# A transformer block in float32 pairs: new instruction orders on five engines, from the first LayerNorm to the first layer-two product

## The reference

```python
h = tok(x)                                    # shifted patches, LayerNorm, 3840 -> 192
h = h + attn(layernorm(h))                    # 12 heads of 16; keys: every 8th token, itself, its predecessor
h = h + ffn(layernorm(h))                     # 8 experts, the two likeliest of a router, 192 -> 768 -> 192
# attention: a = softmax(where(mask, q k^T / 4, -inf)); out = a v; then a 192x192 projection
# experts:   out += w_e * (gelu(x w1[e] + b1[e]) w2[e] + b2[e]),  w = top two of softmax, normalised
```

## Time and profile before

| what | value |
|---|---|
| median of 3 runs | 186.79 us (186.65 to 186.85) |
| the profiled execution: its time, its span | 186.15 us, 184.4 us |
| TensorE products busy | 172.6 us, 94% of the span |
| VectorE busy | 138.7 us, 75% |
| ScalarE busy | 116.1 us, 63% |
| GpSimd busy | 84.0 us, 46% |
| chain that ended last, by engine | PE 63%, DVE 5%, POOL 3% |

### The profile page before, as it was taken

How to read it: one execution, slowest core, us unless ns; L and a number is a source line. 1 busy time by engine, 2 the same in 40 slices (tenths; PEclk the granted TensorE clock), 3 DMA queues, 4 the chain that set the end, 5 groups by cost and what they waited for, 6 DMA issues and landing times.

```text
span 184.4 us, 3458 instructions
## 1 busy us (share of the span) xinstructions
PE 172.6 (94%) x1129; PEld 147.5 (80%) x1129; DVE 138.7 (75%) x311; ACT 116.1 (63%) x208; POOL 84.0 (46%) x111
## 2 busy tenths in 40 slices
PE   5898999698988989899999999999999999999994
PEld 2486589586865659789899899999999999999994
DVE  5479998678359973997787688688688688687553
ACT  2499653585416445756876875875975975973730
POOL 7876403521998216901651651661662562560000
PEclk9999999999999999999999999999999999999999
DMA  5999999100116800054005406406406400000002
GB/s 120 241 334 324 231 243 241 34 2 0 46 42 211 259 5 0 0 164 136 4 0 174 125 0 177 122 2 170 128 0 202 97 2 0 0 4 0 0 0 85
DMA packets 14979, 18.08 MB, mean 98 GB/s; under 512 B 2467, under 2 KB 10776, under 8 KB 14966
## 3 DMA queue, kind: packets, MB, share of 16 engines
q1 hardware_dynamic: 14422, 17.90, 35.5%
q10 hardware_dynamic: 544, 0.03, 0.2%
HBM read 17.14 MB, written 0.39 MB: 95 GB/s over the span
## 4 chain that ended last, share of the span: by engine, by line
PE 63%; DVE 5%; POOL 3%; issue 1%; POOLq 0%; DVEq 0%
PE ps L371 30%; PE ps L1187 18%; PE ps L1189 8%; PE ps L1237 1%; PE ps L1236 1%; PE ps L1235 1%; DVE merge L1268 1%; PE ps L383 1%; DVE big_r L1268 1%; POOL h L589 1%; POOL halo L597 1%; DVE bn L1435 1%; PE ps L378 1%; POOL halo L602 1%; POOL wsplit L330 1%
## 5 line engine op out<-in xcount | busy, mean ns | idle before, releaser
L371 PE MATMUL ps<-big_r,wsplit 128*128 128x512 f32 (+1 forms) x245 | 61.5, 387 | 0.0
L793 ACT ACTIVATE early<-ps,b1t 128x512 f32<-128x512 f32 x48 | 32.8, 683 | 29.1 <-PE ps L371 27.4
L1187 PE MATMUL ps<-wsplit,big_r 128*128 128x384 f32 x168 | 49.7, 355 | 0.7 <-DVE big_r L1268 0.7
L1268 DVE TENSOR_TENSOR big_r<-early,big_r 128x512 fp32r<-128x512 f32 x48 | 35.9, 750 | 15.8 <-ACT big_r L334 15.4
L371 PEld LDWEIGHTS ps<-big_r,wsplit 128*128 128x128 f32 x245 | 41.9, 189 | 6.3
L1189 PE MATMUL ps<-wsplit,big_r 128*128 128x192 f32 x168 | 42.1, 251 | 0.0
L1187 PEld LDWEIGHTS ps<-wsplit,big_r 128*128 128x128 f32 x168 | 31.5, 188 | 2.7 <-issue 1.1
L1189 PEld LDWEIGHTS ps<-wsplit,big_r 128*128 128x128 f32 x168 | 32.0, 190 | 1.3
L334 ACT ACTIVATE big_r<-early 128x512 fp32r<-128x512 f32 x48 | 30.4, 632 | 1.5
L1606 DVE SCALAR_TENSOR_TENSOR merge<-sq,gates,merge 128x192 f32<-128x192 f32 x32 | 26.9, 863 | 0.0
L316 POOL TENSOR_TENSOR wsplit<-stage,wsplit 128x768 fp32r<-128x768 f32 x4 | 7.4, 1848 | 19.3 <-ACT wsplit L334 15.7
(11 more groups left out here) (239 smaller groups left out, 282.0 us busy)
## 6 DMA issues: line engine op xcount, KB each, us to landing
stage<-in_L_ffn_w SPq DMA_DIRECT2D x4, 576.0 KB, 6.2
early<-in_L_ffn_w SPq DMA_DIRECT2D x4, 576.0 KB, 5.3
shifted<-in_L_tok_w SPq DMA_DIRECT2D x6, 288.0 KB, 7.0
early<-in_x SPq DMA_DIRECT2D x6, 256.0 KB, 4.8
stage<-in_L_ffn_w SPq DMA_DIRECT2D x4, 384.0 KB, 3.8
stage<-in_L_ffn_w SPq DMA_DIRECT2D x8, 192.0 KB, 4.8
early<-in_L_ffn_w SPq DMA_DIRECT2D x4, 384.0 KB, 3.1
early<-in_L_ffn_w SPq DMA_DIRECT2D x8, 192.0 KB, 4.2
```

The lines of the kernel that those rows point to most:

```text
L371: mm = nc.tensor.matmul(dst, lhs, rhs, start=(first and n == 0), stop=(last and n == 4))
L793: nc.scalar.activation(gf[:, j % NG], ps[:, HPB[j % 4], :], ACT.Gelu, bias=b1t[:, bass.ds(k, 1)]).then_inc(s_gelu, 1)
L1187: nc.tensor.matmul(ps[:, AB[t], 0:2 * D], g_hi[:, j % NG, tok], w2c, start=(f == 0), stop=False)
L1268: return nc.vector.tensor_tensor(o, a, b, op)
```

## The change

Nothing is computed otherwise. These steps change their place:

- ScalarE rounds parts 0, 1 and 2 of expert 0's weights ahead of `small_high(2)`, which copies a transposed small weight out of PSUM; before, parts 0 and 1 came behind it, and part 2 after the first group's rounding. `values(0)` goes ahead of the second group's column copies and rounding.
- TensorE runs two products of 512 columns whose result nobody reads, ahead of the first group's transposes. The second group's transposes go behind `values(1)`, `masks(0)` and `strided_scores(0)`. `repeated_v(0)` goes ahead of `near_by_heads(1)`, and `transposed_p(1)` ahead of `repeated_v(3)`.
- VectorE spreads group 0's keys ahead of normalising group 1, and takes group 1's scores ahead of group 0's denominators. `low_hidden(0, 0)` goes ahead of `two_largest`; the search for the experts' numbers stands alone (`experts_found`), and the comparison comes behind `low_hidden(0, 2)`.
- GpSimd makes expert 0's layer-two low part and the row sum behind the first group's near values, no longer ahead of them. Expert 1's line 321 waits for the first `low_hidden` (s_glo = 1), its layer-two low part for the third (s_glo = 3) in place of the second.

```diff
@@ -263,6 +263,7 @@
         PTB, PVB, ATB, OB, N2B = (2, 4), (0, 7), (1, 6), (2, 4), (3, 5)
         RB, VBB, RTB = 7, 3, 6
         EARLY = 3
+        IDLE = 2
         LAG = 3
         HPB = [0, 1, 2, 3]
         AB = [4, 5, 6, 7]
@@ -310,7 +311,8 @@
             split_low_w1(pool, e, slot)
             split_low_w2(pool, e, slot)
 
-        def split_low_w1(pool, e, slot):
+        def split_low_w1(pool, e, slot, ready=0):
+
             st, ws = staged[slot], wsplit[slot]
             pool.wait_ge(s_w1hi, e * 2 + 1)
             nc.gpsimd.tensor_tensor(ws[:, W1L:W1L + F], st[:, 0:F], ws[:, W1H:W1H + F].bitcast(F32),
@@ -318,6 +320,8 @@
 
             pool.wait_ge(s_w1m, e + 1)
             pool.wait_ge(s_w1hi, e * 2 + 2)
+            if ready:
+                pool.wait_ge(s_glo, ready)
             nc.gpsimd.tensor_tensor(ws[REM:P, W1R:W1R + F], st[REM:P, F:2 * F],
                                     ws[REM:P, W1R:W1R + F].bitcast(F32), ALU.subtract).then_inc(s_w1lo, 1)
             pool.wait_ge(s_w1lo, e + 1)
@@ -582,12 +586,6 @@
             rstd(0, 1)
             pool.wait_ge(s_nlo, G)
             split_low_w1(pool, 0, 0)
-            split_low_w2(pool, 0, 0)
-
-            pool.wait_ge(s_n, TT)
-            pool.wait_ge(s_row, 1)
-            nc.gpsimd.tensor_tensor(h[:, :, :], h[:, :, :], const_row[:, :].unsqueeze(1).broadcast_to([P, TT, D]),
-                                    ALU.add).then_inc(s_hrow, 1)
 
             def near_values(g):
 
@@ -607,16 +605,23 @@
                 for t in (2 * g, 2 * g + 1):
                     pool.wait_ge(d_prev[t], 16 * len(pieces(1, P)))
                 near_values(g)
+                if g == 0:
+                    split_low_w2(pool, 0, 0)
+                    pool.wait_ge(s_n, TT)
+                    pool.wait_ge(s_row, 1)
+                    nc.gpsimd.tensor_tensor(h[:, :, :], h[:, :, :],
+                                            const_row[:, :].unsqueeze(1).broadcast_to([P, TT, D]),
+                                            ALU.add).then_inc(s_hrow, 1)
             pool.wait_ge(s_nv, G)
             rstd(1, 0)
             rstd(1, 1)
             pool.wait_ge(s_n2lo, G)
-            split_low_w1(pool, 1, 1)
+            split_low_w1(pool, 1, 1, 1)
 
             pool.wait_ge(c_euler, 1)
             pool.wait_ge(s_gsub, 1)
             nc.gpsimd.tensor_tensor(gs[:, 1], euler[:], gs[:, 0], ALU.pow).then_inc(s_gexp, 1)
-            pool.wait_ge(s_glo, 2)
+            pool.wait_ge(s_glo, 3)
             split_low_w2(pool, 1, 1)
 
             with pool.Fori(1, E // 2) as i:
@@ -708,10 +713,11 @@
             small_high(1)
             act.wait_ge(s_mask, 2)
             copy(mask_x[:], mask[:, :].unsqueeze(1).unsqueeze(1).broadcast_to([P, 2, HEADS, NS])).then_inc(s_maskx, 1)
-            small_high(2)
             act.wait_ge(d_stage[0], 16 * STAGE_DMAS)
             split_high(0, 0)
             split_high(0, 1)
+            split_high(0, 2)
+            small_high(2)
 
             def high_parts(g, ps_ready, banks, dst, done):
                 act.wait_ge(ps_ready, g + 1)
@@ -755,13 +761,12 @@
             high_parts(0, s_nt, NTB, nt, s_nhi)
             small_high(3)
             copy(b1t[:], ps[:, WB[3], 400:400 + E * FC]).then_inc(s_wathi, 1)
-            split_high(0, 2)
             split_high(0, 3)
             act.wait_ge(d_bqk, 16 * BQK_DMAS)
             transposed_q(0)
+            values(0)
             last_columns_again(0, 1, n1)
             high_parts(1, s_nt, NTB, nt, s_nhi)
-            values(0)
             act.wait_ge(s_emb, G)
             act.wait_ge(d_stage[1], 16 * STAGE_DMAS)
             split_high(1, 0)
@@ -1104,6 +1109,8 @@
             pe.wait_ge(s_watlo, 2)
             pe.wait_ge(s_bias, 1)
             masks(1)
+            for _ in range(IDLE):
+                nc.tensor.matmul(ps[:, NTB[0], :], xh[:, 0, 0:P], xh[:, 0, :], start=True, stop=True)
             transposes(0, n1, s_n, lambda t: t + 1, NTB, s_nt, s_ndup)
             small_transposes(3)
 
@@ -1126,11 +1133,11 @@
                                       wat[:, part, OUT0:OUT0 + D].bitcast(F32), start=(n == 0), stop=(n == 2))
             mm.then_inc(s_vbias, 1)
             values(0)
-            transposes(1, n1, s_n, lambda t: t + 1, NTB, s_nt, s_ndup)
             values(1)
             pe.wait_ge(s_watraw, 1)
             masks(0)
             strided_scores(0)
+            transposes(1, n1, s_n, lambda t: t + 1, NTB, s_nt, s_ndup)
             near_by_heads(0)
 
             pe.wait_ge(s_nhi, 2)
@@ -1142,15 +1149,15 @@
             values(2)
             values(3)
             strided_scores(1)
+            repeated_v(0)
             near_by_heads(1)
-            repeated_v(0)
             repeated_v(1)
             transposed_p(0)
             near_scores(1)
             strided_values(0)
             repeated_v(2)
+            transposed_p(1)
             repeated_v(3)
-            transposed_p(1)
             transposes(0, ao, s_ao, lambda t: t // 2 + 1, ATB, s_at, s_aodup)
             strided_values(1)
             projection(0)
@@ -1479,8 +1486,8 @@
             with_low_weights(1)
             embedding(1)
             statistics(0, 1, h, s_h, lambda t: t + 1)
+            key_blocks(0)
             normalised(0, 1, h, n1)
-            key_blocks(0)
 
             def near_products(g):
 
@@ -1542,8 +1549,8 @@
             near_products(1)
             v_blocks(0)
             v_blocks(1)
+            scores(1)
             denominators(0)
-            scores(1)
             outputs(0)
             v_blocks(2)
             v_blocks(3)
@@ -1579,9 +1586,11 @@
                 dve.wait_ge(s_gtop, TT)
                 tt(gs[:, 0], top[:, :, 1], top[:, :, 0], ALU.subtract).then_inc(s_gsub, 1)
 
-            def their_experts():
+            def experts_found():
                 for t in range(TT):
                     nc.vector.max_index(topi[:, t], top[:, t], lg[:, t]).then_inc(s_gidx, 1)
+
+            def their_experts():
                 dve.wait_ge(s_gidx, TT)
                 link(nc.vector.tensor_copy(topf[:], topi[:]))
                 iota3 = iota_e[:, :].unsqueeze(1).broadcast_to([P, TT, E])
@@ -1655,11 +1664,12 @@
 
             dve.wait_ge(s_rl, 2)
             nc.vector.tensor_copy(lgt[:], ps[0:E, RB, :]).then_inc(s_rlsb, 1)
+            low_hidden(0, 0)
             two_largest()
-            low_hidden(0, 0)
             low_hidden(0, 1)
+            experts_found()
+            low_hidden(0, 2)
             their_experts()
-            low_hidden(0, 2)
             pair(0, False, first=True)
             with dve.Fori(1, E // 2 - 1) as i:
                 pair(i, False)
```

## The result

The changed kernel takes 183.57 us (median of 4, 183.24 to 184.18), the kernel before beside it 186.72 (186.65 to 186.85); the ratio is 0.983, 95% interval 0.980 to 0.987. The direction was forecast, the size was not: 2.4 us were forecast and 183.57 lies just under the range of 183.7 to 185.6. The 0.66 us above the forecast were won between the first LayerNorm and the residual, most of them in the prediction's term of 1.6 us for the start of `outputs(1)`.

The account below looks back on a forecast made before the run. The end was taken as the first layer-two product's start plus a fixed stream, with GpSimd's chain binding ahead of it; 1.6 + 0.8 = 2.4 us off 186.79 gave 184.4 us, 8-in-10 range 183.7 to 185.6.

Parts of the forecast that it names:

- term of 1.6 us: GpSimd's chain up to group 1's near values: `outputs(1)` begins at 59.4, 1.6 us earlier, and everything behind shifts with it.
- TensorE's new order: Second transposes behind `values(1)`, masks and scores: start only 0.2 us earlier, giving back most gain; GpSimd's expert 0 1.0 earlier.
- First LayerNorm: Group 0: roundings moved into ScalarE's idle 5.21 us gain 1.35 us (1.0 to 1.5); weights may come up to 3 us late.
- Key blocks and near products: VectorE: group 0's key blocks, likelier 0.65 us, leave the near products' way; these end at 43.5 instead of 45.52.
- GpSimd's order: GpSimd from 45.2: near values and sum of group 0 to 51.9, then line 330, row sum, group 1's near values to 59.4.
- The small moves: `repeated_v(0)` and `transposed_p(1)` forward, scores ahead of denominators: costed at nothing; without the cover at most 0.5 us more.
- The gates: First low part ahead of `two_largest` and line 321: TensorE's 0.69 us of idle goes, about 0.8 us gained (0.69 to 0.9).
- the rule weighed there: VectorE and GpSimd: the second to issue blocks until the first finishes; would lower the sum by about 0.1 us; not followed.
- (a): Rival: GpSimd gains less, through meetings with VectorE or a late DMA of 0.5 to 1 us; 185.0 to 185.6; chance 0.20.
- (b): Rival: the 0.2 us margin at chunk 3 breaks, TensorE waits 0.3 to 0.7 us in the experts; 184.7 to 185.1; chance 0.10.
- (c): Rival: TensorE's clock falls between first transposes and second LayerNorm; slower, 5 us of such products make 189.4; chance 0.05.
- (d): Rival: edits cancel, second transposes slip over 0.2 us beyond 43.07, chunk 3's margin breaks too; 186.5 to 187.1; chance 0.07.

Follow-up runs that it names:

- m330: Changed kernel with expert 0's layer-two low part (line 334) moved out of GpSimd's chain to behind the second group's second normalising; 182.53 us.
- u_act: Changed kernel with ScalarE's roundings of expert 0's weights put back behind `small_high(2)`, part 2 behind the first rounding; 185.3 us.
- again: The changed kernel unaltered, run once more; 183.28 us, ratio 0.982.
- late_act: Changed kernel with the four roundings of expert 0's weights moved later, around `transposed_q(0)`; 183.56 us, ratio 0.984.
- b_again: The kernel before, unaltered, profiled once more; 186.66 us, ratio 1.0.
- after: The first profiled execution of the changed kernel, its slowest of four; 184.18 us.
- u_copy: Changed kernel with only ScalarE's copy of the values put back behind the second group's column copies and rounding; 185.77 us over twelve executions.
- u_rest: Changed kernel with `repeated_v(0)`, `transposed_p(1)` and scores ahead of denominators put back; 183.44 us.
- u_tr: Changed kernel with TensorE's second transposes put back ahead of `values(1)` and ScalarE's copy of the values back behind their rounding; 184.49 us.
- tr_mid: Changed kernel with the second group's transposes placed between `values(1)` and `masks(0)`; 183.26 us.
- u_pool: Changed kernel with expert 0's layer-two low part and the row sum put back ahead of both near values on GpSimd; 184.12 us.
- m330_b: The kernel of `m330` run once more; 182.62 us, ratio 0.977.
- u_idle: Changed kernel without the two unread products ahead of the first transposes; 183.53 us.
- two_parts: Kernel before with only expert 0's weights rounded early, the unread products and the gates' new order; 184.13 us.

## Why the prediction was right in its mechanism, and where it failed

**What bounds, and the mechanism: right.** The end is the start of the first layer-two product plus a fixed stream: 99.8 us from chunk 4 in every kernel. The chain through GpSimd is the binding one: `outputs(1)` released by line 600, no gap before it, and `m330` moved the end when it was shortened. What failed is a size: the term of 1.6 us, for all that comes ahead of `outputs(1)`, measured 2.17 there and 2.30 at the residual. Most of what it lacked lies in the step on TensorE's new order.

**First LayerNorm: right.** Predicted 1.35, measured 1.44 (`u_act`). But the allowance for the load was wrong. The prediction read the start of ScalarE's idle time (34.26 - 5.21 = 29.05) as the landing and gave it 3 us; the idle time ended with TensorE, so its row said nothing of the load, which in that profile landed at 31.79. The load lands at 30.0 to 33.7 in these profiles, and it may land no later than some 2.2 us before the normalising, the length of three roundings, or 32.4 in a profile like that of `again`. In six of the seventeen profiles it landed later than that; three of these six have an order in which it costs nothing (`late_act`, `u_act`, `b_again`), and `after`, `u_copy` and `u_rest` lost 0.81, 0.42 and 0.23.

**Key blocks and near products: right.** Near products of group 0 were to end 43.5 - 34.44 = 9.1 behind the normalising; in `again` they end at 43.59, 8.96 behind it, and TensorE, released by them, starts at 43.74 - 34.63 = 9.11.

```profile
41.95 1.64 DVE L1498 SCALAR_TENSOR_TENSOR shifted<-ps,bqk,sq 128x256 f32<-128x256 f32 x4
```

**TensorE's new order: the step that failed, by half a microsecond.** The second transposes start 42.83 - 34.63 = 8.20 behind the normalising, against 42.87 - 34.44 = 8.43 predicted (0.23). Of the 0.23, 0.11 come from the first LayerNorm (1.46 at the first transposes, 1.35 predicted) and 0.12 from the products between, which overlap more closely than the sum of their rows. The transposes then take 0.66 us against 0.91 before. The 0.91 of the earlier trace rows held a wait for the second tile; the new order does away with it, and the prediction carried the distance of 1.55 us from the first transpose to the rounded tile over, where 1.29 remains (0.26). GpSimd thus starts 10.29 behind the normalising, against 45.2 - 34.44 = 10.76: 0.47 of the 0.67 that were missed up to the residual. "Gives back most of the gain on that branch" is too strong: with the transposes early GpSimd starts 11.75 - 9.64 = 2.11 earlier than before (`u_tr`), of which the new place gives back 0.65, and at the end only 0.19 of it counts (`tr_mid`). The prediction said of the shifting DMAs only that they had a slack of 1.0. In `again` they have 2.2, the fourth landing at 46.59 and the near values starting at 48.75, since it takes 2.0 us where 3.6 were allowed; and without the copy's move they are the bound, for 1.4 to 1.6 us, which the prediction did not say.

**GpSimd's order: right in its durations.** From the end of group 0's near values to `outputs(1)` 7.5 us were predicted and 59.05 - 51.52 = 7.53 measured. The part ahead of it, from GpSimd's start to that end, was 0.1 too long (6.7 against 6.60). The term 1.6 measured 26.59 - 24.42 = 2.17 at `outputs(1)`. At the residual it is 2.30, since in the kernel before the residual came 1.20 behind `outputs(1)` and now 1.07; the prediction had that distance unchanged.

**The small moves at nothing: right** (0.05, `u_rest`). The unread products were charged 0.1 and cost nothing.

**The gates: right**, 0.8 predicted and 0.81 measured. The chain is the one described: the difference of the two largest stands still beside line 325 (1.50 us for four numbers, to the end of that instruction), the comparison beside line 334 (2.91), the conversion takes 0.17. Of the rule weighed there: GpSimd's power keeps its 1.30 us from 74.84 while VectorE's low part of 75.75 runs in 0.67, and line 334 follows 0.08 behind that low part, not behind a delay; the 0.1 us of the rule is not there. But the prediction's reading that "the wait fell on GpSimd" has no support either: the power takes 1.30 us in all seventeen profiles, however much of it lies beside a low part, so no wait shows on either engine.

**Rivals.** (a) did not come: near values kept 2.01, and GpSimd has no gap. (b) came in small: the pitch is 2.41 to chunk 3 (76.97 to 79.38 in `again`, behind 2.29 and 2.30), whose low part ends just ahead of its product, and four pitches together take 9.39 against 9.34 before. The margin of 0.2 was in truth just used up, at a price of 0.05 to 0.1, where the rival had 0.3 to 0.7. (c) did not come; it fits the kernel before, see below. (d) did not come, though its sign was there: in the profile of after the second transposes start at 43.70, 0.63 beyond 43.07, by the late landing, and the execution is still 1.97 us faster than that of before.

The sum in the prediction's own terms, from the profiles of before and `again`: 2.26 up to the router's logits (37.08 less 34.82; predicted 1.6) and 0.85 from there to the first product (predicted 0.8), less 0.05 at chunk 3: 3.06.

## What to carry to other kernels

A wait in front of a moved instruction is sized by the row that shows what ended it, and an idle time that another engine ended says nothing of when the load behind it arrived; read the landing itself, over several executions. When work is moved past a wait, the group's own duration changes too: a group of four that held a wait in it shrinks when its inputs are early. An instruction that releases DMAs is judged by what waits for them: the copy of the values, one half microsecond of ScalarE, is worth 1.55 us in the trace of `u_copy`. And a chain that has just been freed shows the next candidate at once: the longest instruction in it that nobody needs there (line 334 for expert 0, 2.6 us) was worth another 0.75 to 0.78.

## What was not expected of the hardware

**The granted clock differs between executions of one kernel.** The profile of the kernel before that the prediction rests on showed the full clock in every slice. In the 60 executions of that kernel beside the experiments, 10 had a mean granted clock of 1.0 (186.14 to 186.74 us, median 186.44), 34 of 0.99 (median 186.47), and 16 of 0.982 (187.50 to 188.21, median 187.88). `b_again` itself adds six, five and one. The first two kinds take the same time, and the four executions beside the first result (186.65 to 186.85) lie below all of the third, so the measured gain owes the clock nothing that shows. The profile of `b_again` is one of the second kind:

```profile
PE   5998999789988979899999999999999999999994
...
PEclk9999999979999999999999999999999999999999
```

and in stretches of it, TensorE's share and its granted clock:

```profile
core 0: us, PE busy (x) PEld busy (x) DVE busy (x) ACT busy (x) POOL busy (x), PEclk, DMA share, GB/s
36.00:40.00 4.00, 2.56 (x16) 2.32 (x17) 1.61 (x6) 3.41 (x9) 1.08 (x2) 0.87 0.01 2
40.00:44.00 4.00, 4.00 (x25) 4.00 (x25) 3.09 (x11) 2.21 (x6) 1.61 (x2) 0.71 0.01 2
44.00:48.00 4.00, 4.00 (x42) 2.76 (x42) 2.69 (x8) 2.94 (x5) 1.49 (x1) 1.00 0.08 22
```

TensorE was busy for 2.56 of the 4 us, its wait for the column copies among the rest, and then the clock was at its lower level (1.2 GHz) for a part of 38 to 44 us. The profile with this fall is only 0.1 us behind that without it (50.31 against 50.20): the second transposes start 9.29 behind the normalising in place of 8.63, but GpSimd's expert 0 starts at the same 11.74, so TensorE is not what binds in that stretch. Elsewhere a fall stands beside a longer time: in `u_act`, `u_pool` and `u_copy` the executions at 0.99 stand 0.9 to 1.3 us above those at full clock (186.2, 184.5 and 185.8 against 185.0, 183.6 and 184.5). How much of that is the clock itself, and how much a longer wait that came with it, is not shown. All three falls that profiles show (`b_again`, `u_pool`, `u_copy`) lie in or behind a stretch in which TensorE idles. But the profile of before has nearly the same stretch (busy 2.89 of the 4 us) and no fall, so what decides is not settled here. The Trainium skill (TensorE: Matmul & The Clock Gate, section "What's actually happening") says that activity releases the throttle; the direction agrees. The changed kernel had 0.998 to 1.0 in its nine executions, `m330` and `m330_b` 0.998 to 1.0 in twelve. So rival (c) was the wrong way round: it is the kernel before that loses the clock, and the change also removes these falls. Which edit does it is settled only so far: with the weights undone it fell in 4 of 10 executions, with GpSimd's order undone in 3 of 6, with the copy of the values undone in 7 of 12, and in none of 6 each with the unread products undone (`u_idle`), with transposes and copy both undone (`u_tr`) and with the weights and the gates alone (`two_parts`).

**A load lands within a span of 3.8 us.** Expert 0's weights were there between 29.99 and 33.74 us over seventeen profiles of fourteen kernels that issue the loads in the same order.
